# Score and maximum matmuls of the second attention on one half of the array each

## The reference

```python
q = (x @ Wq).reshape(b, n, 32, 16)
k, v = jnp.split(ctx @ Wkv, 2, axis=-1)      # each to (b, 512, 32, 16)
q = apply_axial_rope(q, pos_map)
k = apply_axial_rope(k, ctx_pos_map)
logits = jnp.einsum('bqhd,bkhd->bhqk', q, k) * scale
w = jax.nn.softmax(logits, axis=-1)
attn = jnp.einsum('bhqk,bkhd->bqhd', w, v)
return attn.reshape(b, n, 512) @ Wout + bout
```

## Time and profile before

| | us |
|---|---|
| median of 3 runs | 1985.25 |
| lowest and highest run | 1985.19, 1998.39 |
| profiled execution, device time | 2002.5 |
| its span, first to last instruction | 2000.8 |
| projection stage, from the first fill to the last split | 531.9 to 701.0 |
| second attention, first fill to last normalisation | 728.0 to 1181.4 |

### The profile page before, as it was taken

The page is one execution under the profiler, slowest core; times in us unless marked ns, Lnnn a source line. Parts: engine busy times, 40 slices in busy tenths (PEclk is TensorE's granted clock), DMA queues, the critical chain, the costliest instruction groups (busy, mean ns, idle before and its releaser), DMA issues. The chain is left out here.

```text
span 2000.8 us, 29937 instructions
## 1 busy us (share of the span) xinstructions
PE 1719.9 (86%) x8915; PEld 1303.1 (65%) x8915; DVE 1163.5 (58%) x2119; ACT 785.5 (39%) x1242; POOL 375.2 (19%) x339
## 2 busy tenths in 40 slices
PE   7886799996096828999999988889999968999997
PEld 6775799996085614555555546667777846777785
DVE  6876422223764628888888835555555555555555
ACT  5553233332132205666666662333333323333332
POOL 1110122321132343000000000032222303222221
PEclk9998799999597958999999999899999989999998
DMA  8873155623526645433333300101111021011101
GB/s 295 302 272 128 48 215 205 255 78 107 182 85 205 201 146 178 109 79 86 86 84 77 77 1 14 43 20 40 39 39 39 1 75 28 20 40 39 39 20 42
DMA packets 172093, 202.21 MB, mean 101 GB/s; under 512 B 60560, under 2 KB 115856, under 8 KB 168160
## 3 DMA queue, kind: packets, MB, share of 16 engines
q1 hardware_dynamic: 146896, 169.56, 27.5%
q0 software_dynamic: 6384, 20.98, 3.1%
q10 hardware_dynamic: 18720, 10.49, 2.1%
HBM read 260.23 MB, written 74.32 MB: 167 GB/s over the span
## 5 line engine op out<-in xcount | busy, mean ns | idle before, releaser
L1842 DVE TENSOR_REDUCE r_top<-r_ring 128x1 f32<-128x512 f32 x512 | 330.7, 686 | 41.3 <-PE r_ring L1741 39.0
L1826 ACT ACTIVATE r_probs<-r_st 128x1024 f32<-128x1024 f32 x256 | 248.3, 1022 | 131.9 <-PE r_st L1730 128.8
L2404 POOL TENSOR_TENSOR f_hidS<-f_work,f_hidS 128x512 fp32r<-128x512 f32 x132 | 170.6, 1293 | 424.7 <-ACT f_hidS L2364 424.7
L1741 PE MATMUL r_ring<-r_kM,r_qS 128*128 128x512 f32 x512 | 206.1, 443 | 46.3 <-DMA r_v<-v_pad 42.5
L1741 PEld LDWEIGHTS r_ring<-r_kM,r_qS 128*128 128x128 f32 x512 | 99.1, 194 | 133.2 <-DVE r_top L1842 70.3
L2521 DVE TENSOR_TENSOR f_work<-f_work,f_u 128x512 f32<-128x512 f32 x132 | 90.8, 688 | 135.5 <-PE f_u L48 75.9
L48 PE MATMUL m_bank<-w_place,m_xT 128*128 x936 | 165.9, 326 | 3.3 <-DVE m_xT L1189 3.3
L1730 PE MATMUL r_st<-r_qS,r_kM 128*128 128x512 f32 x512 | 161.2, 398 | 0.0
L48 PEld LDWEIGHTS m_bank<-w_place,m_xT 128*128 128x128 f32 x936 | 151.3, 188 | 7.2 <-issue 3.9
L2359 ACT ACTIVATE f_work<-f_g 128x512 f32<-128x512 f32 x132 | 78.9, 598 | 182.6 <-PE f_g L56 125.5
L2364 ACT ACTIVATE f_hidS<-f_work 128x512 fp32r<-128x512 f32 x132 | 83.3, 631 | 171.1 <-DVE f_work L2521 171.1
(11 more groups left out here) (344 smaller groups left out, 2832.1 us busy)
## 6 DMA issues: line engine op xcount, KB each, us to landing
w_place<-expert_split SPq DMA_DIRECT2D x72, 1408.0 KB
w_place<-expert_split SPq DMA_DIRECT2D x36, 1024.0 KB
expert_split<-w_place SPq DMA_DIRECT2D x10, 1408.0 KB, 9.2
w_place<-expert_split SPq DMA_DIRECT2D x36, 384.0 KB
r_qS<-q_stack SPq DMA_DIRECT2D x64, 200.0 KB
q_stack<-q_qkT SPq DMA_DIRECT2D x48, 256.0 KB
k_stack<-q_qkT SPq DMA_DIRECT2D x48, 256.0 KB
r_kM<-k_stack SPq DMA_DIRECT2D x64, 192.0 KB
```

The costliest lines, as they stand in the source:

```text
L1741: nc.tensor.matmul(ring(place(q, h))[:], qS[s][:, h // 2, q * P:(q + 1) * P], kM[s][:, h, :], start=True, stop=True).then_inc(max_ready, 1)
L1826: nc.scalar.activation(probs[k][:, 2 * pair:2 * pair + 2, :], st_ps[pair][:], ACT.Exp, scale=SCALE).then_inc(exp_done, 1)
L1842: nc.vector.reduce_max(top[s % 2][:, q, h:h + 1], ring(place(q, h))[:], AXIS_X).then_inc(max_read, 1)
L2404: nc.gpsimd.tensor_tensor(hidS[c][:, var, LO, :], hid(c, var), fp32(hidS[c][:, var, HI, :]), ALU.subtract).then_inc(hid_split, 1)
```

## The change

The maximum and the score matmul of a head now take only the rows in which the head lies: 48 rows for maxima and 50 for scores, from row 0 for the even head and from row 64 for the odd one. `kM` therefore holds two heads in a column, as `qS` does, and is half as large. The zero rows, the zeros in `kM` and the zero DMA are gone; `set_slot` fills only the ones. `q_stack` has 48 rows a head.

The order of the stream changes: the two maximum matmuls of a pair stand next to each other, and so do the pairs' score matmuls. `maxima` takes a pair and waits for the banks of both heads ahead of the first matmul.

```diff
-        kM = [sb(f"kM{s}", [P, GROUP, S], FP32R) for s in range(RING)]
+        kM = [sb(f"kM{s}", [P, GROUP // 2, S], FP32R) for s in range(RING)]
...
-        CONST_ROWS = 6
+        CONST_ROWS = 2
...
-            done = 0
-            for half in halves:
-                tail = slice(64 * half + 32, 64 * half + 64)
-                other = slice(64 * (1 - half), 64 * (1 - half) + 64)
-                for rows, value in ((qS[s][tail, :, :], 0.0), (kM[s][tail, half:GROUP:2, :], 1.0),
-                                    (kM[s][other, half:GROUP:2, :], 0.0)):
-                    memset(fp32(rows), value).then_inc(slot_set_pool if halves == (1,) else slot_set[s], 1)
-                    done += 1
-                    each(done)
+            for done, half in enumerate(halves):
+                rows = kM[s][64 * half + 32:64 * half + 64, :, :]
+                memset(fp32(rows), 1.0).then_inc(slot_set_pool if halves == (1,) else slot_set[s], 1)
+                each(done + 1)
...
                 for j in range(2):
-                    last = nc.tensor.matmul(st_ps[pair][:, j, :], kM[s][:, 2 * pair + j, k * P:(k + 1) * P],
-                                            qS[s][:, pair, :], start=True, stop=True)
+                    rows = slice(64 * j, 64 * j + QROWS)
+                    last = nc.tensor.matmul(st_ps[pair][:, j, :], kM[s][rows, pair, k * P:(k + 1) * P],
+                                            qS[s][rows, pair, :], start=True, stop=True)
                 last.then_inc(scores_ready, 1)
 
-            def maxima(g, i, s, q, heads):
-
-                for h in heads:
-                    if q == 0 and h == 0:
-
-                        pe.wait_ge(kqv_in[s], (i + 1) * LOADS * DMA)
-                    bank_free(g, place(q, h))
-                    nc.tensor.matmul(ring(place(q, h))[:], qS[s][:, h // 2, q * P:(q + 1) * P], kM[s][:, h, :],
+            def maxima(g, i, s, q, pair):
+
+                if q == 0 and pair == 0:
+
+                    pe.wait_ge(kqv_in[s], (i + 1) * LOADS * DMA)
+                for j in range(2):
+                    bank_free(g, place(q, 2 * pair + j))
+                for j in range(2):
+                    rows = slice(64 * j, 64 * j + KROWS)
+                    nc.tensor.matmul(ring(place(q, 2 * pair + j))[:], qS[s][rows, pair, q * P:(q + 1) * P], kM[s][rows, pair, :],
                                      start=True, stop=True).then_inc(max_ready, 1)
...
-                    maxima_of(0)
-                    scores(g, i, s, k, 0)
-                    maxima_of(1)
-                    scores(g, i, s, k, 1)
-                    maxima_of(2, 3)
+                    for pair in range(2):
+                        if left >= 2:
+                            maxima(g + 2, i + (s + 2) // RING, (s + 2) % RING, k, pair)
+                        scores(g, i, s, k, pair)
```

More of the change, by code:

```diff
@@ L1229, in dram @@
         return nc.dram_tensor(name, shape, dt, kind="Internal").ap()
-    return {"q": dram("q_stack", [B * HEADS, QROWS, S], FP32),
+    return {"q": dram("q_stack", [B * HEADS, KROWS, S], FP32),
             "k": dram("k_stack", [B * HEADS, KROWS, S], FP32),
@@ L1299, in phase_qkv1 @@
         vpad = [sb(f"vpad{i}", [P, HEADS, PAD]) for i in range(2)]
-        zeros = sb("zeros", [P, 2, S])
         n = TokenNorm(nc, ctx, "qn", stats)
@@ L1311, in phase_qkv1 @@
             sem("qk_ready"), sem("rope_done"), sem("rot_done"), sem("v_ready"), sem("v_copied"))
-        pads_set, out_zero = sem("pads_set"), sem("out_zero")
+        pads_set = sem("pads_set")
         out_q = [sem("out_q0"), odd.stored]
@@ L1337, in _ @@
                 sp.wait_ge(out_v[i], START + TILES // 2 * DMA)
-            sp.wait_ge(out_zero, DMA)
         @block.tensor
@@ L1405, in _ @@
             nc.scalar.activation(wkv[:, HI], wkv_raw[:], ACT.Copy).then_inc(wkv_hi, 1)
-            act.wait_ge(pads_set, 5)
+            act.wait_ge(pads_set, 4)
             with act.Fori(0, B // 2) as pair:
@@ L1450, in _ @@
                 nc.gpsimd.memset(vpad[i][:], 0.0).then_inc(pads_set, 1)
-            nc.gpsimd.memset(zeros[:], 0.0).then_inc(pads_set, 1)
-            pool.wait_ge(pads_set, 3)
+            pool.wait_ge(pads_set, 2)
             for i in range(2):
                 nc.gpsimd.memset(vpad[i][:, :, HD:HD + 1], 1.0).then_inc(pads_set, 1)
-            pool.dma_start(scr["q"][:, 3 * HD:QROWS, :], zeros[:]).then_inc(out_zero, DMA)
             pool.wait_ge(wkv_hi, 1)
@@ L1651, in load @@
                     heads = slice(half, GROUP, 2)
-                    sp.dma_start(fp32(kM[s][rows:rows + KROWS, heads, :]),
+                    sp.dma_start(fp32(kM[s][rows:rows + KROWS, :, :]),
                                  scr["k"][ds(g * GROUP, GROUP), :, :][heads].rearrange("h r n -> r h n")).then_inc(kqv_in[s], DMA)
-                    sp.dma_start(fp32(qS[s][rows:rows + QROWS, :, :]),
+                    sp.dma_start(fp32(qS[s][rows:rows + KROWS, :, :]),
                                  scr["q"][ds(g * GROUP, GROUP), :, :][heads].rearrange("h r n -> r h n")).then_inc(kqv_in[s], DMA)
@@ L1778, in _ @@
                 for q in range(KT):
-                    maxima(g, 0, g, q, range(GROUP))
+                    for pair in range(2):
+                        maxima(g, 0, g, q, pair)
                     if (g, q) == (1, 0):
@@ L1784, in step @@
                 for k in range(KT):
-                    def maxima_of(*heads):
+                    for pair in range(2):
                         if left >= 2:
-                            maxima(g + 2, i + (s + 2) // RING, (s + 2) % RING, k, heads)
-                    maxima_of(0)
-                    scores(g, i, s, k, 0)
-                    maxima_of(1)
-                    scores(g, i, s, k, 1)
-                    maxima_of(2, 3)
+                            maxima(g + 2, i + (s + 2) // RING, (s + 2) % RING, k, pair)
+                        scores(g, i, s, k, pair)
                     if k == 0:
```

## The result

| | before | after |
|---|---|---|
| median, timed side by side (20 runs each) | 1997.79 us | 2006.93 us |
| ratio after to before | | 1.0055, 95% interval 1.0033 to 1.0076 |
| profiled execution: span, mean clock | 2000.8 us, 0.932 | 2002.7 us, 0.927 |

The account below looks back on a forecast made before the run. The prediction took the cycle through TensorE and VectorE over the ring of three PSUM banks as the bound. Terms 4.8 - 1.6 - 0.4 - 1.5 = +1.3 us on a median of 1985.25 gave 1987 us, range 1970 to 2050.

Parts of the forecast that it names:

- the first maxima: Entry of the second attention: the first 16 maxima, in pairs, take 13.1 us where they took 11.3, +1.8 us.
- the ring: Second attention's PSUM banks: the second maximum pair waits each step for head 0's read; group 13.24 against 13.08, +4.8 us.
- The pair: Maximum and score matmuls on two row halves: full overlap, a pitch of 0.23 us a pair.
- Rival 1: Second attention: the two halves of a pair don't overlap, each pair takes 0.46 us; 2043 us, chance 0.19.
- Rival 2: Second attention: a pair's two weight loads go one after the other when exposed, +12 us; 1999 us, chance 0.12.
- Rival 3: Second attention: the time saved on TensorE counts; 1920 us in full, 1953 us for a half, chance 0.09.
- The size of the steps: A group's four steps in the second attention: 3.58, 3.50, 3.25 and 2.91 us, together 13.24.
- The layouts: Array layout changes in a step: 0.09 us each, 0.19 with the exposed load behind the shifts' and outputs' turns.
- The last two groups: End of the second attention, groups without maxima: steps of 1.97 us where they took 2.24, in all -1.6 us.
- The fills: Entry of the second attention: VectorE fills once instead of three times before the first load, -2.2 us.
- rival 4: Second attention: gaps in each step keep TensorE's clock at 0.5, about 4.5 us a step; some 2190 us, chance 0.04.
- The projection stage: Projection stage: zero rows (0.5 MB) no longer written to DRAM, between 0 and -2.0 us, -1.5 taken.

Follow-up runs that it names:

- e1: The changed kernel with VectorE reducing only the first 256 of 512 keys of each maximum; period 12.16 us a group, ratio 0.988 to the kernel before.
- e4: The kernel before (full 128 rows) with the changed kernel's step order and its wait for both banks of a pair; period 14.87 us, ratio 1.0336.
- e5: The changed kernel in its own order, but each maximum matmul waits for its own bank alone; period 13.24 us, ratio 1.0042 to the kernel before.
- e2: The kernel before with VectorE reducing only the first 256 of 512 keys of each maximum; period 12.89 us a group, ratio 0.9933.
- e3: The changed kernel's row halves with the step order and single waits of the kernel before; period 12.53 us, ratio 0.9926 to the kernel before.

## Why the prediction was right or wrong

The mechanism that was to decide, the second pair's wait for the read of head 0, came as forecast. The sum failed in three terms: the first maxima (+1.8 taken, +4.4 measured), the ring's +0.16 us a group (0.26 measured, +4.8 taken where it is +7.8), and the clock at the entry, which was put at nothing (+2.8 from the first score to the first output).

**The pair: right.** A pitch of 0.23 us a pair was taken, and the score pair's stream begins 0.23 behind the maximum pair's (991.63 to 991.86); the pair's row is 0.50 us, like one matmul's. Rival 1 (no overlap, 2043 us) falls. Rival 2 (the second weight load behind the first, +12) falls too: the loads of a pair stand in one row of 0.19 us, as a single one does in the earlier trace rows.

```profile
992.81 0.19 PEld L1735 LDWEIGHTS r_ring<-r_kM,r_qS 48*128 48x128 f32 x2 [0.98 <-DVE r_top L1832]
```

**The ring: the mechanism was right, and it was the deciding term.** The plain step was to lose 0.12 and lost 0.08 (3.03 to 2.95); all the rest of the saved 0.92 went into the new wait, and e1 to e4 bear it out. The Trainium skill says in "TensorEngine Tiling (Array Packing)", PSUM Bottleneck, that tiling speeds up TensorE but not the emptying of PSUM. The trace agrees: TensorE is 78 us less busy and waits longer (161.5 us in the stage, before 58.2) for reads of an unchanged 0.69 us. Rival 3, for which the page's theoretical speedup spoke, falls: neither 1920 nor 1953 came. One sign was off: VectorE reads in fours, 2.56 us, and not in twos: the second pair's matmuls end at 993.31, just before the second read does (992.06 + 1.29).

**The size of the steps: this term failed.** The plain step, 2.91, was mis-sized by 0.04, as were two of the other three. Streams of the first pair begin at 984.81, 988.34, 991.63, 994.58 and 998.17 (record start + 0.10), so by the steps' names:

| step | forecast | measured |
|---|---|---|
| with the shifts turned (994.58 to 998.17) | 3.58 | 3.59 |
| with the outputs turned | 3.50 | 3.54 |
| behind the normalisation | 3.25 | 3.29 |
| plain | 2.91 | 2.95 |
| group | 13.24 | 13.36 |

The plain step by its parts: the second pair begins 1.29 behind the first (992.81 - 991.52, forecast 1.27), and the next step's first pair 1.67 behind that (994.48 - 992.81, forecast 2.91 - 1.27 = 1.64). No link was missing; several had each been taken 0.01 or 0.02 too short, and they follow each other in every step. Against 13.08 the plain groups of the loop have 13.34, so 30 x 0.16 should have been 30 x 0.26 = +7.8.

**The layouts: right.** From the shifts' turn to the next stream it is 0.63 (984.17 to 984.80, forecast 0.63), and the values' load stands 0.11 behind the end of the score pair's stream (993.14 + 0.23 = 993.37 to 993.48; forecast 0.09).

**The groups that aren't plain: left out.** The stream is a loop of four groups a turn, with four groups written out ahead of it and four behind. The first group of a turn is 13.73 us after the change (0.40 more than the others) and 13.27 before (0.19 more): 0.21 in each of five turns, +1.0. The three groups ahead of the loop and the two behind it that still have maxima grew not by 0.26 but by 0.54 to 0.64 each (13.53 against 12.98 ahead of the loop), +1.5 beyond 5 x 0.26. Against it the loop's first group is 0.40 shorter, 13.47 against 13.87. The causes weren't tried.

**The last two groups: right.** From the end of the last maximum to the last output it is 22.13 us, before 23.25: -1.1, forecast -1.6.

**The fills: right.** -1.9, forecast -2.2.

**The first maxima: this step failed.** The prediction had +1.8 for the first group's 16 and nothing for the second's, since they "lie beside the wait for the third group's loads, which ends about 764". Two errors. The pitch of pairs isn't 1.57 everywhere: where a place of the ring is skipped for the shifts or the outputs, a pair needs the bank of the second head of the pair before, and it is 2.23. So the first 16 took 732.08 to 746.79 = 14.7 us (forecast 13.1), before 11.3: +3.5. And the end of the wait isn't a fixed time. The cover was there before: TensorE waited 3.55 us for the load, with the second group's maxima done. But SyncE issues that load only behind the first group's shifts, so what the first 16 lose is passed on; and with pairs the second group's maxima take longer than the load, so that after has no wait for it left:

```profile
764.29 0.80 PE L1741 MATMUL r_ring<-r_kM,r_qS 128*128 128x512 f32 x1 [3.55 <-DMA r_v<-v_pad]
```

```profile
762.48 0.79 PE L1735 MATMUL r_ring<-r_kM,r_qS 48*128 48x512 f32 x2 [0.85 <-DVE r_top L1832]
```

From the end of the first 16 reads to this matmul it is 14.7 us before and 15.7 after, +1.0. Sum +4.4. e4 has the same with full rows: 14.7 for the first 16, 15.8 to the third group's first maximum, 31.5 to the first score. e5, without the pair's wait, has 11.2 and 14.3, a wait of 2.78 us for the load again, and 26.2. In e2, half reads shorten the first 16 to 8.7 us, the load is issued the sooner, and the first score follows on it again, after 22.1.

**The clock at the entry: not forecast in this form.** The prediction feared a clock that stays low in the stage (rival 4); with TensorE busy for 309.99 of 389 us it was granted 1.00 throughout. But it rose at 776.84 in after and at 770.09 before. Before had even been at 1.00 from 756.44 to 763.26, within the first maxima, which the earlier trace rows doesn't show and the prediction missed:

```profile
758.00:760.00 2.00, 1.70 (x4) 0.59 (x4) 2.00 (x4) 0.00 (x0) 2.00 (x2) 1.00 0.74 179
```

From the first score on, 13.8 us passed at 1.2 GHz in after and 5.2 before, and between first score and first output it is +2.8. That the clock is the cause was argued, not tried; it fits that in after a step took 4.68 us at 1.2 GHz (771.11 to 775.79) and the next, with the rise in it, 3.33, and that in e5 25.0 us passed at 1.2 GHz and the first output came 28.0 us behind the first score. Ahead of the rise after had gaps of 0.8 to 1.5 us in front of nearly every pair, before had fewer. How much of the delay is the change and how much is chance stays open: the rise stood at 768.85 to 783.17 us in the other kernels on halves, and it was latest in e5, whose first maxima have fewer gaps than after's and whose TensorE was busy for all of the 14 us from 763 to 777 at a granted clock of 0.50.

**The projection stage: not to be told.** -1.5 was forecast and -3.7 is in the pair of profiles. But the eight profiles without the zero rows, whose code is the same up to there, have 189.6 to 204.3 us for this mark, and the four with them 195.9 to 211.4. The rows of GpSimd's first fills in after and in e1 (same code, 12 us apart):

```profile
531.26 1.84 POOL L1448 MEMSET q_vpad<- 128x1024 f32 x2 [43.76 <-POOLq L2558]
...
723.67 6.96 POOL L1622 MEMSET r_kM<- 32x1024 f32 x7 [31.32 <-POOLq L1272]
```

```profile
531.97 1.84 POOL L1448 MEMSET q_vpad<- 128x1024 f32 x2 [43.60 <-POOLq L2558]
...
736.29 6.96 POOL L1622 MEMSET r_kM<- 32x1024 f32 x7 [34.63 <-POOLq L1272]
```

**The sum** by what was measured. First to last output is +7.7: the 29 groups with maxima from there on grew by 9.3 together, of which 0.3 lies ahead of the first output, and the last groups shrank by 1.3, counted here from the last `TENSOR_SCALAR`. With +4.4 for the first maxima, +2.8 for the clock and -1.9 for the fills it is +13.0, or +10.2 without the clock's part; the ratio gives +11. That the two meet so nearly is in part luck, since one profile on each side can't tell the projection stage or the clock. The mechanism in the stage was right. The entry (+1.8 that was +4.4, and a clock put at nothing) and the rounding in a sum taken 120 times were not.

## What to carry to other kernels

Before a busy engine is made faster, write down the cycle through its partner: here the four matmul streams saved in a step turned into a wait for one read, and the same halves were worth 1.1 us a group as soon as independent work (the values) stood in that wait. When matmuls are paired, look at what is queued behind the pair's wait, and give each its own where nothing else fills the wait. In a chain that repeats in every step keep the third decimal, and read the entry of a stage with the same care as its steady state: a wait that ends "about 764" has an issuer, and what the change delays ahead of the issuer moves its end.

## What the hardware showed that was not expected

- Two matmuls of 48 rows in the two halves of the array, issued one behind the other, have a common row of 0.50 us, and their loads of 128 columns one of 0.19 us: here neither the streams nor the exposed loads of the halves held each other up.
- One idle time of 2.43 us of TensorE in the stage was followed by 7 us at 1.2 GHz (e3), while idle times of 0.5 to 0.9 us in every step (after) left the clock at 2.4 GHz for the 389 us of the window.
- The time from the projection stage's first fill to the second attention's differed by 15 us between kernels with the same code there. In 637 to 644 us the granted clock was 1.00 in after and 0.52 in e1; that this makes the difference wasn't tried:

```profile
637.00:644.00 7.00, 6.42 (x31) 5.05 (x30) 4.11 (x9) 1.47 (x3) 2.71 (x2) 1.00 0.58 211
```

```profile
637.00:644.00 7.00, 6.01 (x21) 4.80 (x19) 2.04 (x4) 1.74 (x4) 0.00 (x0) 0.52 0.52 193
```
